# Cross-attention on one core: the ring of transposed probabilities holds three units, before it held four

## The reference, cut to what matters

```python
qh, kh, vh = heads(x @ Wq), heads(context @ Wk), heads(context @ Wv)   # 8 heads of 128, 2048 tokens each
sim = qh @ kh.T * SCALE; mean = sim.mean(-1)
attn = softmax((sim - mean) * 1.5 + mean)        # 2048 x 2048 for each head
out = (attn @ vh) -> 2048 x 1024 -> @ Wout + bout
```

## Time and profile before

| | |
|---|---|
| median of 3 runs | 1335.51 us (1335.32 to 1337.71) |
| the profiled execution, its own time | 1338.53 us |
| its span, first to last instruction | 1336.5 us |
| mean granted TensorE clock | 0.989 |
| busy in the span | PE 1294.0, DVE 1025.0, POOL 907.9, ACT 895.8 us |

### The profile page before, as it was taken

One profiled execution on the slowest core, in us unless ns is written; L12 is line 12 of the kernel. 1 busy time (PEld: TensorE's weight loads), 2 busy tenths in 40 slices (PEclk: granted clock), 3 DMA queues, 4 the chain that ended last, 5 costly groups with the idle time before them and its releaser, 6 DMA issues. The chain is left out here.

```text
span 1336.5 us, 22731 instructions
## 1 busy us (share of the span) xinstructions
PE 1294.0 (97%) x8358; PEld 1078.1 (81%) x8358; DVE 1025.0 (77%) x1628; ACT 895.8 (67%) x1315; POOL 907.9 (68%) x645
## 2 busy tenths in 40 slices
PE   5999999999999999999999999999999999987998
PEld 4677788888877788888888888888888888776998
DVE  6354498849306889989999999999999999985554
ACT  5555433325646878877878878778787777765774
POOL 2544420125410899989989999999999989863553
PEclk9999999999999999999999999999999999997999
DMA  6702032146773998988888888888888888786572
GB/s 220 103 6 73 3 96 83 37 131 256 210 242 124 247 221 219 225 197 214 220 200 215 216 196 222 215 197 219 214 203 215 204 191 209 183 246 241 194 237 78
DMA packets 172377, 241.35 MB, mean 181 GB/s; under 512 B 34179, under 2 KB 78085, under 8 KB 172272
## 3 DMA queue, kind: packets, MB, share of 16 engines
q1 hardware_dynamic: 155040, 208.11, 61.8%
q10 hardware_dynamic: 15184, 25.96, 5.6%
q0 software_dynamic: 2048, 5.90, 1.1%
HBM read 64.79 MB, written 41.32 MB: 79 GB/s over the span
## 5 line engine op out<-in xcount | busy, mean ns | idle before, releaser
L1217 POOL TENSOR_TENSOR xa_pT<-xa_moved,xa_pT 128x1024 fp32r<-128x1024 f32 x246 | 586.8, 2410 | 26.5 <-ACT xa_pT L1735 25.1
L1557 PE MATMUL xa_S<-xa_kT,xa_qT 128*128 128x512 f32 x1536 | 388.9, 401 | 1.8 <-ACT xa_probs L1741 1.2
L1741 ACT ACTIVATE xa_probs<-xa_S,xa_mx_nb_rinv 128x1024 f32<-128x1024 f32 x256 | 285.8, 1117 | 147.2 <-DVE xa_mx_nb_rinv L1339 147.2
L1574 PE MATMUL xa_O<-xa_pT,xa_v 128*128 128x512 f32 x1536 | 378.5, 395 | 3.0 <-DVE xa_pT L1392 2.6
L1336 DVE TENSOR_REDUCE xa_mx_nb_rinv<-xa_S 128x1 f32<-128x1024 f32 x256 | 305.4, 1211 | 79.5 <-PE xa_S L1557 79.5
L1574 PEld LDWEIGHTS xa_O<-xa_pT,xa_v 128*128 128x128 f32 x1536 | 290.2, 189 | 70.2 <-DVE xa_pT L1392 2.9
L1557 PEld LDWEIGHTS xa_S<-xa_kT,xa_qT 128*128 128x128 f32 x1536 | 288.4, 188 | 68.5 <-ACT xa_probs L1741 2.5
L1349 DVE STREAM_TRANSPOSE xa_tq<-xa_probs 128x1024 f32<-128x1024 f32 x256 | 316.7, 1238 | 13.5 <-ACT xa_probs L1741 5.9
L1735 ACT ACTIVATE xa_pT<-xa_moved 128x1024 fp32r<-128x1024 f32 x254 | 253.8, 1050 | 2.3 <-PE xa_O L1574 1.7
L506 PE MATMUL fw_pp<-fw_hT,fw_wqk 128*128 128x512 f32 x384 | 99.0, 408 | 4.3 <-DVE fw_hT L647 4.3
L506 PEld LDWEIGHTS fw_pp<-fw_hT,fw_wqk 128*128 128x128 f32 x384 | 71.8, 193 | 20.6 <-DVE fw_hT L647 3.0
(11 more groups left out here) (247 smaller groups left out, 1698.1 us busy)
## 6 DMA issues: line engine op xcount, KB each, us to landing
xa_moved<-xa_tq SPq DMA_DIRECT2D x508, 256.0 KB, 4.6
heads_k<-ci_outs SPq DMA_DIRECT2D x32, 256.0 KB, 2.2
heads_v<-ci_outs SPq DMA_DIRECT2D x32, 256.0 KB, 2.3
heads_q<-ci_outs SPq DMA_DIRECT2D x32, 256.0 KB, 2.4
xa_chunk<-heads_v ACTq DMA_DIRECT2D x32, 256.0 KB, 4.0
ex_w1s<-in_L_ffn_w_dram SPq DMA_DIRECT2D x8, 1024.0 KB, 7.5
ex_w2s<-in_L_ffn_w_dram SPq DMA_DIRECT2D x8, 1024.0 KB, 9.5
xa_chunk<-heads_q ACTq DMA_DIRECT2D x31, 256.0 KB, 4.2
```

Source lines behind the costliest of these rows:

```text
L1217: pool.tensor_tensor(quadrants(pT[LO], r), unit_moved(r), quadrants(pT[HI], r).bitcast(F32), ALU.subtract).then_inc(lo_ready, 1)
L1557: last = pe.matmul(banks[:, k % 2], qT[a][:, i // GT % 2, q], kT[b][h % 2][:, k * 512:(k + 1) * 512], start=(n == 0), stop=(n == 2))
L1574: last = pe.matmul(O[:], v[a][:, j * P:(j + 1) * P], pT[b][:, r % PRING, k], start=(j == 0 and n == 0), stop=(j == JT - 1 and n == 2))
L1741: act.activation(probs[:, unit % RING], S[:, score_banks(unit)].rearrange("p a b -> p (a b)"), ACT.Exp, bias=nb[:, s % 2:s % 2 + 1], scale ...
```

## The change

One constant becomes three. It sets three things: the number of places in the two `xa_pT` tiles, the place of a unit (`r % PRING`, in `quadrants` and in the operands of L1574), and the count that ACT waits for ahead of a high part: the wait for unit `r - 4` becomes one for unit `r - 3`.

```diff
-        CRING, RING, MRING, PRING = 2, 2, 3, 4
+        CRING, RING, MRING, PRING = 2, 2, 3, 3
         HALF = TOK // 2
...
         pT = [home(f"xa_pT{a}", "pT", [P, PRING, 2, GCOLS], F32R, a * 4 * 2 * TOK) for a in (HI, LO)]
```

## The result

The changed kernel takes 1344.44 us (median of 5 runs, 1342.64 to 1348.57); the kernel before, timed beside it, 1337.71 (5 runs, 1335.32 to 1340.24). The ratio is 1.0061, 95% interval 1.0043 to 1.0079: slower by 0.6%. By the ratio that is 0.0061 x 1337.71 = 8.2 us, by the medians 6.7; the forecast was 11.4. The profiled execution took 1342.64 us around a span of 1340.6, with a mean granted clock of 0.992.

The account below looks back on a forecast made before the run. PE was taken as the bound, 97% busy with no idle in the steady cross-attention; 10.9 + 0.15 + 0.3 = 11.4 us on 1335.51 gave 1347 us, range 1341 to 1355 (8 in 10).

Parts of the forecast that it names:

- Item 1: PE's second scores unit of the next slot: 0.13 us of room left at its load, so cost 0.
- Item 2: Copy of `xa_O` at group ends: PE's load 0.62 us late, 0.52 us paid at 21 ends, 10.9 us, plus 0.15.
- the 0.84 passes through whole: ACT from first exponential to next slot's high part runs back to back, so its 0.84 us lateness reaches the copy undiminished.
- item 4: SP's moves into `xa_moved` and ACT's chunk loads get later but are wanted slots later: cost 0.
- Item 3: POOL's low parts start later by 0.84 us at most, against 1.06 us of room where POOL is latest: cost 0.
- POOL becomes late: Rival: two waits in one pair idle POOL, PE waits in most chunk slots, 8 us more, 1355; chance 0.05.
- Item 5: After the last scores, the second high part and the router's copies wait too: between 0 and 1 us, taken as 0.3.
- Not slower: Rival: ACT's idle ahead of the exponentials swallows the move, time stays 1335.5; chance 0.09.
- Scores: Rival: a longer wake-up makes PE's scores wait as well, in some 29 even slots, 1357 or 1353; chance 0.10.
- Clock at the new stalls: Rival: PE's clock falls at all 21 stalls, 28 us more, 1375; chance 0.02.
- The 230 us of waits on ACT: ACT waits for PE ahead of L1735 in nearly every slot, 1.7 to 2.2 us each, some 230 us in all.

Follow-up runs that it names:

- the wait alone: Kernel before, ring kept at four places, but ACT waits for unit r - 3 as with three: 1347.98 us, ratio 1.0079.
- one, four and eight small copies: Kernel before, with one, four or eight tiny ACT copies into an unused tile ahead of the group-end copy: 1337.49, 1339.60, 1344.70 us.
- its copy moved in two ways: Changed kernel, group-end copy put between the two exponentials of the slot before (1339.68 us), or behind both, ahead of the chunk's high part (1338.12 us).
- the mended one: Changed kernel, with the copy ahead of the chunk's high part and the output weights' load one slot sooner: 1334.82 us, ratio 0.9982.
- the two single runs on the end: Kernel before, with the wait of a ring of three only from unit 230, or only from unit 244: 1333.37 and 1334.55 us, one run each.

## Why the prediction was right, and where its sizes were off

**What bounds the kernel, and the wait (right).** PE was the bound and had no room: of the 0.56 us by which a load is late, all but the 0.10 to 0.11 of the restart arrives in the group's length. The late chain, ACT's second high part behind unit 2p, passes through two exponentials and the chunk to the copy. The kernel with the wait alone shows its start, those that move or delay only the copy show its end; the steps between are read from the ACT rows of slot 34.

**Item 1, the scores (right).** No wait of L1557 for L1741 in the steady part, with three places. That the room was small is shown by two places, where they wait 87 times.

**Item 2, the copy (right in kind and count, too large in size).** A stall was put at 0.52 us and is 0.45. The push itself held: the first exponential starts 0.96 behind the high part (608.97 to 609.93), where 0.95 was reckoned. What failed is the step behind it, "the 0.84 passes through whole": it took over the spacing of two exponentials where the first has waited for the bias, 609.77 to 610.92 = 1.15. Behind a high part that spacing is 1.09 (609.93 to 611.02), so the copy ends 613.22 - 608.93 = 4.29 us behind unit 2p's end (607.38 + 1.55, by the six matmuls of the earlier trace rows) and not 4.36. 21 x 0.07 = 1.5 us of the sum. The seven group ends without a chunk, put at nothing, pay 0.04 in six cases (24.44 for 24.40): 0.2. The copy in head 0, put at 0.15, has a wait of 0.2 by the load, and the group behind it takes 24.80 for 24.79. 20 of the 21 lie between the second and the twenty-ninth copy: 20 x 0.45 + 0.2 = 9.2, and with the output weights of item 4 9.6, of 9.7 measured.

**Item 3, POOL (right, and closer than it looked).** PE doesn't wait for the low parts from 500 to 1100 us. But the rival "POOL becomes late" is the one with the steepest price: with the second high part moved behind the exponentials the 27 groups take 43 us more than before, and from 500 to 1100 us 29.4 of PE's waits are for POOL and 15.8 for the copy. The order on ACT, high parts ahead of the exponentials, is what protects it.

**Item 4, transfers (wrong in one of them).** I priced the moves and the chunk loads and forgot that SP's list also has the load of the output weights, which waits for the projections of the head before. It is late by a fraction of a microsecond already before the change: 1.1 us of waits in three places from 500 to 1100 us. After it, 1.4 in two. The two groups in which they lie take 24.30 and 24.29 where 23.81 is usual, and took 23.68 and 23.59 where 23.36 was, so about +0.4 us of the 9.7; with the copy moved the same load costs about 3 us, and once it is a slot sooner these are gone. By which step three places delay it no run here separates.

**Item 5, after the last scores (wrong in sign).** Forecast +0.3; measured -1.4. The waits that I walked through are there, but the clock does not fall behind the idle at the router, and that is worth more.

**The sum.** 11.4 less 1.5 for the stall's size, less 0.1 for head 0, plus 0.2 for the ends without a chunk, plus 0.4 for the weights, less 1.7 at the end gives 8.7, as the table does; the ratio gives 8.2. The 1341 to 1355 held. That 1344.4 lies so near 1347 is in part luck: the kernel before took 1335.51 in the runs that the forecast stood on and 1337.71 beside the changed one. From there it would have been 1349.1, and the miss in the difference is 3.2 us of 11.4.

**The rivals.** Not slower: it falls, ACT's idle swallows only a part, as reckoned. It comes true once the copy and the weights are moved. Scores: falls. POOL: falls for this change. Clock at the new stalls: it falls, too. The granted clock from 500 to 1100 us is 1.00, with 18 stalls of 0.6 us in it. The rule of the Trainium skill that the prediction weighed ("TensorE: Matmul & The Clock Gate", "A second HAM failure mode: psum-queue depth-cycling") is not borne out by these rows.

**What would show it.** Groups with a chunk at the end take 24.34 us (515.22 to 539.56), as foretold about 24.4; the bias wait is gone; PE waits for the copy 21 times for 0.6 us, as foretold, and once for 0.2. The 230 us of waits on ACT were too many: 169.3 in all. I had multiplied a slot's largest waits by the slots; a slot with an output projection on PE or little idle on ACT waits less. Not foretold: DVE's transposes wait for ACT, 35.2 us in 49 times. It costs nothing, since DVE has some 60 us of idle in 600 and the transposes are wanted slots later.

## What to carry to other kernels

When a ring gets a place less, don't ask only whether the engine that fills it has time; list everything that stands behind the new wait on that engine's list, down to the rarest instruction, and compare each with the time at which someone needs it. Most of the cost was in one small copy in every fourth slot, 4.3 us behind the wait, and two thirds of it went by exchanging this copy with its neighbour. And once such a stall is mended, look at what was just in time beside it: here the next was a load of weights, which in the changed kernel had shown only 1.4 us of waits, and 4.3 to 4.6 once the copy was in time.

## What the runs showed of the hardware that was not expected

An idle of the same length at the same place, with the same matmuls ahead of it, does not always bring TensorE's clock down. In all five profiles in which the last slots wait as for four places (the kernel before, one, four and eight small copies, the weights sooner) the stretch behind the router's idle of 2.1 us takes 15.0 to 15.1 us, its first 5.5 us have a granted clock of 0.69, and 128x512 matmuls there are spaced at 0.43 us for 2 to 3 us where they are otherwise at 0.23: near the lower of the two levels, 1.2 for 2.4 GHz. In seven that wait as for three places at least in the last six slots and have the same idle (the wait alone, the changed kernel, its copy moved in two ways, the mended one, the two single runs on the end) it takes 13.7 to 13.8 us at a granted clock of 1.00. Nor does a longer idle bring it down: with a ring of two the idle there is 3.1 us, with the second high part behind the exponentials 1.3, and both have 1.00 behind it. That makes it no accident of one run, but why it is so isn't settled. What differs in the kernels is the count that ACT waits for in the last slots; by which step that reaches the clock no run here shows.
